# A two-layer vision tower on one core: the last network's first group of tiles moved into the second attention's last tiles, banks shared anew, and orders changed in both layers

## What is computed

```python
h = h + _L0_attn_ref(_layernorm(h), Wq, Wk, Wv, Wo)      # weights 1 + s + s*s/2, causal, 16 heads
h = h + _L0_ffn_ref(_layernorm(h), weight, bias, ...)    # 4-bit block quantised, 256 -> 256
h = h + _L1_attn_ref(_layernorm(h), Wq, bq, ..., bo)     # softmax, causal, 16 heads
h = h + _L1_ffn_ref(_layernorm(h), U1, V1, b1, U2, V2, b2)
# the last:  P = x @ U1; H = gelu(P @ V1 + b1); Q = H @ U2; y = Q @ V2 + b2   (256 -> 64 -> 1024 -> 64 -> 256)
```

## Time and profile before

| | |
|---|---|
| median of 3 runs | 323.95 us (322.25 to 326.37) |
| the profiled execution | 326.31 us, its span 324.6 us |
| PE busy | 270.3 us (83%) |
| DVE busy | 215.1 us (66%) |
| ACT busy | 151.4 us (47%) |
| POOL busy | 171.7 us (53%) |
| chain that ended last | PE 43%, DVE 28%, issue 9%, POOL 6%, ACT 6%, SP's queue 4%, DMA 3% |

### The profile page before, as it was taken

The page is one execution under the profiler, slowest core; times in us unless marked ns, Lnnn a source line. Parts: engine busy times, 40 slices in busy tenths (PEclk is TensorE's granted clock), DMA queues, the critical chain, the costliest instruction groups (busy, mean ns, idle before and its releaser), DMA issues.

```text
span 324.6 us, 6978 instructions
## 1 busy us (share of the span) xinstructions
PE 270.3 (83%) x2720; PEld 209.0 (64%) x2720; DVE 215.1 (66%) x389; ACT 151.4 (47%) x313; POOL 171.7 (53%) x238
## 2 busy tenths in 40 slices
PE   1779899679997979798779749888999956799893
PEld 1668788558876858587668638777888844333331
DVE  0626375116698998999869998999999991422121
ACT  2312111469886858676236515543555442143541
POOL 7233335134677797979756566476776631601000
PEclk9999999799999999999979998999999995579998
DMA  6798500000000000000000000000000000001011
GB/s 178 185 267 253 128 1 3 0 0 5 2 0 2 2 2 2 1 5 0 2 0 2 2 1 3 3 0 2 0 2 2 3 0 0 3 0 31 27 60 38
DMA packets 9742, 9.87 MB, mean 30 GB/s; under 512 B 4037, under 2 KB 8878, under 8 KB 9710
## 3 DMA queue, kind: packets, MB, share of 16 engines
q1 hardware_dynamic: 9294, 9.42, 10.8%
q10 hardware_dynamic: 416, 0.01, 0.1%
HBM read 8.18 MB, written 1.25 MB: 29 GB/s over the span
## 4 chain that ended last, share of the span: by engine, by line
PE 43%; DVE 28%; issue 9%; POOL 6%; ACT 6%; SPq 4%; DMA 3%; ACTq 0%; POOLq 0%; DVEq 0%
PE psum L1236 8%; PE psum L1272 5%; DVE big L1073 5%; PE psum L1489 3%; PE psum L1603 3%; PE psum L1434 3%; DMA img<-in_x 3%; DVE img L988 3%; PE psum L1614 3%; SPq L323 2%; DVE st L942 2%; DVE xq L1029 2%; PE psum L1587 2%; DVE big L981 2%; PE psum L1504 2%
## 5 line engine op out<-in xcount | busy, mean ns | idle before, releaser
L1272 PE MATMUL psum<-hnT,a 128*128 128x114 f32 x352 | 50.7, 289 | 3.3 <-ACT mT L679 1.8
L1272 PEld LDWEIGHTS psum<-hnT,a 128*128 128x128 f32 x352 | 44.7, 198 | 10.1 <-ACT mT L679 4.0
L458 POOL TENSOR_SCALAR ve<-mvs 114x1 f32<-114x1 f32 x44 | 19.9, 452 | 44.4 <-DVE mvs L944 43.3
L798 ACT ACTIVATE big<-psum 114x456 f32<-114x456 f32 x44 | 22.0, 551 | 37.2 <-PE psum L1489 37.1
L1073 DVE SCALAR_TENSOR_TENSOR big<-ex,imgmask,z 114x608 f32<-114x608 f32 x33 | 34.5, 1098 | 0.4
L451 POOL TENSOR_TENSOR big<-mT,headmask 128x456 f32<-128x456 f32 x22 | 21.4, 991 | 23.9 <-ACT mT L649 23.9
L1236 PE MATMUL psum<-wT,patchT 128*114 128x256 f32 x132 | 31.8, 394 | 1.6 <-DVE patchT L898 0.8
L459 POOL TENSOR_TENSOR rstd<-ve,nhalf 114x1 f32<-114x1 f32 x44 | 30.6, 696 | 3.7
L479 POOL TENSOR_TENSOR big<-big,img 114x912 f32<-114x912 f32 x11 | 22.4, 2038 | 15.4 <-ACT big L713 15.4
L1489 PE MATMUL psum<-ident,big 114*114 114x114 f32 x176 | 22.8, 276 | 8.0 <-DVE big L1073 7.3
L1236 PEld LDWEIGHTS psum<-wT,patchT 128*114 128x114 f32 x132 | 23.8, 186 | 6.8 <-DVE patchT L898 2.1
(11 more groups left out here) (158 smaller groups left out, 575.9 us busy)
## 6 DMA issues: line engine op xcount, KB each, us to landing
img<-in_x SPq DMA_DIRECT2D x6, 576.0 KB, 10.5
out<-h_all SPq DMA_DIRECT2D x10, 114.0 KB
w_raw<-in_L_tok_W SPq DMA_DIRECT2D x1, 768.0 KB, 5.9
a_raw<-in_L_attn_Wq SPq DMA_DIRECT2D x1, 256.0 KB, 8.9
a_raw<-in_L_attn_Wk SPq DMA_DIRECT2D x1, 256.0 KB, 9.0
a_raw<-in_L_attn_Wv SPq DMA_DIRECT2D x1, 256.0 KB, 9.2
a_raw<-in_L_attn_Wo SPq DMA_DIRECT2D x1, 256.0 KB, 12.7
qw<-in_L_ffn_weight SPq DMA_DIRECT2D x1, 256.0 KB, 12.8
```

The lines of the kernel that those rows point to most:

```text
L798: nc.scalar.activation(pT[:, 4 * g:4 * g + 4, :], PTB[g % 2][0:T, 0:4 * T], ACT.Copy).then_inc(L["p"], 1)
L1272: return nc.tensor.matmul(bk[:, m * T:(m + 1) * T], w[:, c, m * 128:(m + 1) * 128], hnT[:, c, :], start=(c == 0), stop=(c == DC - 1))
```

## The change

Three parts of the code change, and no arithmetic does.

1. The last network's group 0 (tiles 0 to 3) is done inside `attention()`: its normalisations in tiles 6 and 7, its transposes in tiles 8 and 9, `low(0)` and `up_pair(0, 0)` in tile 9, and the rest in tile 10. The normalisations of group 1 go into tile 9. Waits of the whole stage fall away, and each step waits for its own inputs and banks. After the loop the stage goes on with groups 1 and 2 as before.
2. Banks: the quantised values are turned into bank 7 rather than 4, so `k_proj0` and `m_proj` need no wait for them, and the gelu's inputs get banks by pair (`UPS`).
3. Orders. In layer 0: DVE masks ahead of `quantised` in odd tiles; PE and ACT turn and take the pair in the even tile that follows, behind `sums0` and `take_z`; ACT's `ffn_norm` goes behind `take_k0` or `take_m`, and `attn_norm(2)` ahead of `take_v(1)`. In attention: DVE's `grid`, `scales` and `quantised` of the last two pairs move behind `spread`, or a tile ahead, `residual` goes ahead of `ffn_residual`, and POOL rounds the last pair one tile earlier.

The diff, cut to its core:

```diff
-        X16 = [bank[4].bitcast(bf16), bank[6].bitcast(bf16)]
+        X16 = [bank[7][:, D:2 * D].bitcast(bf16), bank[6].bitcast(bf16)]
...
-        YY = [bank[3], bank[2]]
-        UP = [bank[0], bank[1], bank[4], bank[2]]
-        XX = [bank[6], bank[7]]
+        YY = [bank[3], bank[7]]
+        UPS = [(bank[4], bank[6] if p < FC // 2 else bank[2]) if p % 2 == 0 else (bank[0], bank[1])
+               for p in range(FC // 2 * -(-NT // 4))]
+        XX = [[bank[6], bank[6] if t0 == 0 else bank[7]] for t0 in range(0, NT, 4)]
...
@@ pool, attention @@
+                    if t == 2:
+                        round_to_grid(NP - 1)
+                        add_ffn_bias(NP - 1)
                     if t == 3:
                         rstd_f_step(NT - 3)
-                        round_to_grid(NP - 1)
-                        add_ffn_bias(NP - 1)
...
@@ scalar, layer0 @@
                     take_z(t)
+                    if t >= 4 and t % 2 == 0:
+                        take_xT((t - 4) // 2)
                     if t + 1 < NT:
                         add_one(t + 1)
-                    if t > 0:
-                        ffn_norm(t - 1)
                     i = t + 2 - NT
                     if i < 0:
                         take_k0(t + 2)
+                        if t > 0:
+                            ffn_norm(t - 1)
                         take_v0(t + 2)
                     else:
...
                         take_m(lay[1], i)
+                        if i == 0:
+                            ffn_norm(t - 1)
                         if i == 1:
                             weigh(lay[1], 0)
+                            attn_norm(i + 1)
                         take_v(i)
...
+                    if t == NT - 1:
+                        ffn_norm(t - 1)
...
-                    if t >= 3 and t % 2 == 1:
-                        take_xT((t - 3) // 2)
...
@@ scalar, attention @@
                     if t + 2 < NT:
                         take_m(L, t + 2)
+                    if t == NT - 2:
+                        act.wait_ge(ld_f, 16 * FFN_LOADS)
+                        take_low(0)
                     take_pT(L, t, 2)
                     take_pT(L, t, 3)
...
+                    if t == NT - 1:
+                        gelu(0, 2)
+                        gelu(0, 3)
                     take_oT(L, t)
+                    if t == NT - 2:
+                        gelu(0, 0)
+                        gelu(0, 1)
+                    if t == NT - 1:
+                        for f in range(4, FC):
+                            gelu(0, f)
+                        take_low2(0)
...
@@ vector, layer0 @@
                     if t >= 3 and t % 2 == 1:
+                        mask_weights(t + 1)
                         quantised((t - 3) // 2)
-                        if t + 1 < NT:
-                            mask_weights(t + 1)
...
@@ vector, attention (new; before: ffn_residual ahead of residual, grid ahead of spread, scales(NP - 1) in t == 2) @@
+                    if t + 1 < NT:
+                        keep(t + 1)
+                    if t == NT - 2:
+                        take_pairs(0, 2, 4)
+                    if t == 0:
+                        residual0(NT - 1)
+                        ffn_residual(NT - 4)
+                    else:
+                        residual(t - 1)
+                    if t == 2:
+                        quantised(NP - 2)
+                    if 3 <= t <= 5:
+                        ffn_residual(NT - 6 + t)
+                    if t + 1 < NT:
+                        spread(t + 1)
+                    if t + 2 < NT:
+                        take_v(t + 2)
+                    if t == 0:
+                        scales(NP - 2)
+                    if t == 1:
+                        grid(NP - 2)
+                        scales(NP - 1)
+                    if t == 2:
+                        grid(NP - 1)
+                    if t == 3:
+                        quantised(NP - 1)
+                    if t == 6:
+                        ff_norms(0, 0, 2)
+                    if t == 7:
+                        ff_norms(0, 2, 4)
+                    if t == NT - 3:
+                        take_pairs(0, 0, 2)
+                    if t == NT - 2:
+                        ff_norms(1)
+                residual(NT - 1)
+                take_pairs(1)
...
@@ tensor @@
-            def k_proj0(t, turned=0):
+            def k_proj0(t):
...
-                ge(pe, f_xT, turned)
...
@@ tensor, turn_quantised @@
                 if p < NP - 2:
-                    pe.wait_ge(lay[0]["s_sb"], min(2 * p + 6, NT))
-                    ge(pe, lay[1]["s_sb"], 2 * p + 6 - NT)
+                    pe.wait_ge(lay[0]["h"], 2 * p + 4)
+                    ge(pe, f_h, 2 * p)
...
@@ tensor, layer0 @@
                     sums0(t)
+                    if t >= 4 and t % 2 == 0:
+                        turn_quantised((t - 4) // 2)
...
-                    if t >= 3 and t % 2 == 1:
-                        turn_quantised((t - 3) // 2)
...
@@ tensor, attention @@
+                    if t == NT - 2:
+                        ff_turn(0, 2, 4)
+                    if t == NT - 1:
+                        up_pair(0, 1)
...
                     turn_p(L, t, 1)
...
+                    if t == NT - 2:
+                        pe.wait_ge(ld_f, 16 * FFN_LOADS)
+                        low(0)
+                    if t == NT - 1:
+                        down_pair(0, 0)
+                        up_pair(0, 2)
                     turn_p(L, t, 2)
                     turn_p(L, t, 3)
...
                     values(L, t)
+                    if t == NT - 2:
+                        up_pair(0, 0)
+                    if t == NT - 1:
+                        down_pair(0, 1)
+                        up_pair(0, 3)
...
+                    if t == NT - 3:
+                        ff_turn(0, 0, 2)
+                    if t == NT - 1:
+                        down_pair(0, 2)
                     out_proj(t)
+                down_pair(0, 3)
+                ff_turn(1)
+                low(1)
+                ff_out(0)
```

223 lines of the change are left out of this document (99 added, 124 removed).

## The result

The changed kernel takes 307.4 us (median of 4 runs, 306.47 to 308.57), the kernel before 323.1 us (4 runs beside it, 322.06 to 326.37). The ratio is 0.95 with a 95% interval of 0.9417 to 0.9583. The forecast was 309.5 us. The profiled execution of the changed kernel took 306.47 us, with a span of 304.7 us, against 326.31 and 324.6 before. Some executions of a kernel take over 1.5% more than its fastest: they are left out of the medians here, but the profiled executions of the kernel before, of the run with attention's pairs put back and of the run with DVE's order in layer 0 put back are such.

The account below looks back on a forecast made before the run. DVE bound layer 0 and attention's first six tiles, PE the next three, then a hollow stretch and a PE-ACT chain. Gains 2.1 + 2.2 + 1.6 + 8.5 = 14.4 us off the 323.95 median gave 309.5 us, range 302 to 318.

Parts of the forecast that it names:

- (A): Layer 0: DVE masks before forming quantised values in odd tiles, so the mask escapes POOL in tile 3; 2.1 us gained.
- (B): Seam of the layers: ACT copies the map before the norm, so `scores(1)` starts earlier; 2.2 us, bounds 1.2 and 2.8.
- (C): Attention tiles 0 to 5: `grid` behind spread keeps POOL's rounding off the spreads; 1.6 us gained, bounds 0 and 4.
- (D): Attention tiles 6 to 8: work added to DVE and PE in a saturated place costs 0.9 us.
- (E): Attention tiles 9 and 10 and the last network's first group: `low(1)` begins earlier; 8.5 us, bounds 2.4 and 10.2.
- I cost that at nothing: Layer 0: moving the quantised pair's transposes into the even tile ends PE's waits but was priced at no gain.
- The serial piece of ACT: Tile 10: ex stands behind a copy, `low(0)`, its copy and two more copies, 4.1 us in all.
- The 1.7 us taken off for the clock: Tile 10 and the first group: one stretch at PE's lower clock, 1.7 us off the 10.2 us gain.
- The rival with a clock that stays low: Tile 10 and the first group: PE meets the half clock again, gain 2.4, time 315.7 us; chance 0.2.
- the one in which the lock moves on: Layer 0 and attention's first tiles: DVE still meets POOL; gains 0.5 and 0 there, time 312.7 us; chance 0.22.
- The slower one: Both layers: the pair's transposes delay PE in six places; over 2% slower needs 3.5 us in each; chance 0.03.
- the signs that would have shown the prediction wrong: Attention's first tiles still 11 us each, tile 10's clock 0.5 throughout, or `turn_quantised` waits over 2 us in layer 0.

Follow-up runs that it names:

- three big runs: Changed kernel with layer 0 and the seam, attention's pairs, or the last network put back as before, one at a time: 315.56, 308.71 and 314.36 us.
- the mask's own run: Changed kernel with only DVE's order in layer 0 put back, quantised values ahead of the mask in odd tiles: 310.33 us.
- all four edits: Changed kernel plus earlier bias adds, earlier first group, pairs' transposes behind `v_proj`, and residual ahead of `keep` in tiles 1 and 2: 302.47 us.

## Why the prediction was right, and where only in its sum

The sum was 14.4 us, and the medians differ by 15.7. The three big runs that put parts back confirm the size: 8.2, 1.3 and 7.0 us, 16.5 together. But the parts were not each right. In the traces (A) to (E) gave 5.2 us more than forecast, and a stretch that had no term took 2.0 back; part of the 5.2 us is that the profiled execution of before was a long one. So the number owes something to luck, and in (A) and (C) the gain came by another way than the one told.

- **(A), layer 0, 2.1 us; 2.9 in the traces, 2.9 by the mask's own run.** The size was near, the mechanism was not. Tile 3 gave 1.31 us where 1.4 stood, and tiles 5 and 7 gave 0.43 each where 0.35 stood; the other 0.7 came in tiles 1 and 2 from ACT's copy of k, which the prediction gave nothing. But the mask did not escape POOL: in tile 3 it took 1.85 us and not 1.08, the quantised values 2.44 and not 0.68. The gain of tile 3 was DVE's idle 0.58 us, which the mask filled, 0.3 us less of stretch, and the division's 0.39. And "I cost that at nothing", said of the transposes, is the step that failed: with the mask first, leaving them where they were costs 11.5 us. The order of DVE made the quantised values end later in their tile, by 1.1 us in tile 3 and 2.1 in tile 5, and PE's queue had a whole tile behind them. Costing the two edits one by one could not find this.
- **(B), the seam, 2.2 us; 3.2 in the traces, 3.2 by the run.** Right in mechanism: 2.1 us of earlier start and the whole 1.1 us of `scores(1)`'s clock, of which half was counted. The stated upper bound of 2.8 was too low: it counted only the two named delays, while PE's start came forward by 0.4 us more.
- **(C), attention's first tiles, 1.6 us; 2.1 in the traces, 1.3 by the run.** The size was near, the place was not. The spreads shrank as forecast and PE's 4.65 us behind them went, but the sum 2.05 + 1.26 was not gained: the rounding met `scales(5)` (1.7 us, priced at 1.25), PE waited 5.55 us for the turned values of pair 4, not "about 1 us more", and came back slow, and DVE then waited 0.45 and 1.70 us for PE. `keep(1)` to `keep(4)` took the same time. The gain came in tiles 3 to 5 from the last pair, which no term named. That the 5.55 us cost nothing by themselves nearly held (0.4 us), but for another reason than the one given: PE had no room, DVE was late with everything that PE needed.
- **(D), tiles 6 to 8, cost 0.9 us; 0.6.**
- **(E), tiles 9 and 10, 8.5 us with (D); 11.4 in the traces, 10.1 up to `low(1)` against the run with the last network put back.** The serial piece of ACT was as forecast (11.2 and 12.6 us against 10.67 and 12.25). The 1.7 us taken off for the clock were not due in the profiled execution, whose clock was 1.00 throughout. They were in two others that have the same steps there (with layer 0 and with attention's pairs put back): `low(0)` took 3.25 and 3.37 us, and `keep(10)` to `low(1)` 24.4 and 24.5 us where it takes 22.9. The rival with a clock that stays low fell.
- **"From `low(1)` on the program is the same 30.1 us."** This sentence failed. It was 32.08. The steps were the same but their neighbours were not: POOL's two adds had run over 13 us ahead of `low(1)`, and with the first group's work gone from that place they fell on DVE's last normalisations. Moving the adds gave back 2.3 us.

Of the rivals, the one in which the lock moves on was half right: the collisions did change partners, in layer 0, on `scales(5)` and behind `low(1)`. The slower one, transposes that hold PE up, happened at one place (5.55 us) instead of six. Of the signs that would have shown the prediction wrong none came, but the first was a weak one: attention's first tiles take 10.65 us each, where 11.0 was to be the failure and the forecast itself meant 10.75.

## What to carry to other kernels

Two edits of order on two engines that touch the same value are one edit: cost them together, and ask of each alone what the other engine would then wait for. When work leaves a place, look at what stays behind it in the queues of the other engines and now stands closer to the steps that follow, even where the program after it is the same; here an add on POOL did. If a wait is taken away and nothing is gained, look whether the engine that released it is the bound: then only taking work from that engine helps. And look in which tiles a gain lies before calling its cause the one that was forecast.

## What the runs showed of the hardware

Ahead of layer 0's tiles all kernels here run the same work, but PE's clock between 60 and 72 us differs from execution to execution. The windows of that stretch, first of the kernel before, then of the changed one:

```profile
60.00:72.00 12.00, 9.33 (x71) 7.75 (x74) 1.11 (x1) 6.61 (x15) 2.85 (x2) 0.86 0.00 0
```

```profile
60.00:72.00 12.00, 9.33 (x136) 7.56 (x134) 1.94 (x2) 8.35 (x17) 3.07 (x2) 1.00 0.00 1
```

The counts differ since the slower execution has got less far by 72 us. The clock was 0.86 also in the runs with the bias adds moved, with DVE's order in layer 0 put back and with all four edits, 0.81 and 0.79 in those with layer 0 and attention's pairs put back, and 1.00 in the other six. The first division begins at 72.4 to 73.3 us where the clock was 1.00 and at 74.3 to 75.8 where it was lower, so some 3 us of a difference between two single profiles of this kernel are no effect of an edit. Why one execution keeps the clock and another doesn't wasn't found out.

A half clock also followed some short gaps, and not others of the same length. Ten of the thirteen profiled executions have PE waiting 1.85 us (one of them 1.86) for a residual in attention tile 1. In six of them `values` then takes 0.99 us, in four 1.75. One of each, the kernel before and the run with the pair's transposes behind `v_proj`:

```profile
183.36 0.99 PE L1504 MATMUL psum<-big,vX 114*32 114x114 f32 x32 [1.85 <-DVE h_all L1083]
```

```profile
175.36 1.75 PE L1520 MATMUL psum<-big,vX 114*32 114x114 f32 x32 [1.85 <-DVE h_all L1102]
```

With DVE's order in layer 0 put back, waits of 3.06 and 2.24 us were followed by the half clock and one of 2.63 us was not. So no length that decides can be read from these rows, and that the four transposes in the kernel before kept the clock up by splitting the gap is likely but not shown.
